# A Mamba scan and a mixture of experts on one core: the shared expert moved from 128-token tiles after the scan into the scan itself

## The chip, the cores and the metric

One core of a Trainium2 chip runs the program. The metric is the device time of one launch in microseconds; the kernel before takes 2628.02 us (median of 2 runs, 2627.62 to 2628.42). The engines are PE (TensorE, with its weight loads as PEld), DVE (VectorE), ACT (ScalarE), POOL (GpSimd) and SP (SyncE, which here only issues transfers). Each works through its own instructions in order and waits on semaphores.

## What is computed

```python
x = x + conv_ref(_ln_c(x), ...)     # Mamba: in_proj, 4-tap conv, scan over 2304 steps with 16 states, gate, out_proj
t = _to_tokens(x)                   # 4 images x 24 x 24 pixels = 2304 tokens of 512 channels
t = t + ffn_ref(_ln_t(t), ...)
# ffn: 8 experts (512 -> 1024 -> 512), the best two of each token, and one shared expert for all tokens
h1 = jnp.einsum('th,ehi->tei', xf, w1)
h3 = jnp.einsum('th,ehi->tei', xf, w3)
act = jax.nn.silu(h1) * h3
y = jnp.einsum('tei,te,eih->th', act, combine, w2)
shared = jnp.einsum('tni,nih->th', jax.nn.silu(s1) * s3, sw2)
return y + shared
```

All of it is float32.

## The kernel before

**The scan.** The sequence is cut into 24 chunks of 96 pixels (4 images, 6 chunks each; `g` is the chunk, `j` its place in the image, `b` the image). A chunk has 16 states, `n` = 0 to 15, and each engine's program walks over them. For one `n` ACT makes the decay `dA` (L868), DVE multiplies two halves of `dtu` with the spread B (L1110, L1112) and scans both halves (L1126), POOL multiplies with C (L612), and PE adds pairs of states into `Yt` (`add_pair`, L1454). B is spread by PE into two PSUM banks in turn (`spread`, L1444): the spread for pair `ph` + 2 stands in PE's program at `n` = 2 `ph` + 1, and DVE needs it at `n` = 2 `ph` + 4. Between these the program puts, at fixed `n`, the work of neighbouring chunks: the front half of chunk g + 1 and g + 2 (`dt_product`, `z_first`, `u_first`, `projections`, on ACT the silus at `n` = 2, `bc_hi` at 4 and `exps` at 7) and the back half of chunks g - 1 to g - 3 (`out_product`, the residual, layer norm, `row_transposes`, `gate_logits`). So the order on every engine is written out by hand in five functions named `batch`, one for each engine; ACT may run up to six states ahead of DVE (`AHEAD`), POOL up to six behind (`HRING`).

**The tiles.** After the last chunk the tokens are worked through in tiles of 128 rows with PE (L1581 up, L1593 down): first 18 tiles of all tokens in order with the shared expert's weights, then 43 tiles of rows gathered for the eight routed experts (`RTT` = 43, `NT` = 61). During the shared tiles DVE works out the routing (`softmax_and_greater`, `choose`, `weights_of_the_two`, `places`, `tables`), and POOL scatters the slots with 48 indirect transfers (L647). The shared tiles write their rows to `yrows`, the routed ones add to these rows (L678). At the end `yrows` is loaded, transposed and added to `X`, the residual, in SBUF.

The queue of SP carries nearly all transfers. In a chunk it issues, in this order, C, dt, the finished rows and dtu of the next chunk, each behind a wait of its own.

## Time and profile before

| stage of the profiled execution | us | granted clock (1.00 = 2.4 GHz) |
|---|---|---|
| set-up, until the first product for the scan | 93.9 | |
| scan of 24 chunks | 1105 | 0.77 to 0.85 |
| to the first shared tile | 24.4 | 0.64 |
| 18 shared tiles | 403.9 | 0.99 |
| 43 routed tiles | 956.3 | 1.00 |
| sum, transposes, output | 42.7 | 0.56 |
| span | 2626.3 | 0.884 |
| time of this execution | 2628.03 | |

The span runs from the first to the last instruction; 1.7 us lie around it. In the trace a float32 matmul stands as two instructions. Busy times of PE contain the filling and draining of matmuls that overlap, so a busy PE isn't necessarily at its limit.

### The profile page before, as it was taken

The page shows a single profiled execution, that of the slowest core. Times are in us where ns is not written, and L with a number is a line of the kernel's source. Part 1 is how long each engine was busy: PE and PEld are TensorE (multiplying, and loading weights), DVE is VectorE, ACT ScalarE, POOL GpSimd, SP SyncE. Part 2 cuts the span into 40 slices and gives each one's busy share as a digit, 9 for nine tenths or more (in the row PEclk, how much of TensorE's full clock was granted, in tenths as well). Part 3 has the DMA queues.
Part 4 walks back from the last instruction along what each step waited for, and adds up shares of the span by engine and source line. Part 5 has one row for each costly group of instructions (what it writes and reads, how often), then busy time and mean ns, then how long its engine had stood idle before and what let it go on. Part 6 is the DMA issues. An engine that isn't in the chain of part 4 may idle for free.

```text
span 2626.3 us, 28836 instructions
## 1 busy us (share of the span) xinstructions
PE 2252.7 (86%) x7604; PEld 1074.3 (41%) x7605; DVE 1312.3 (50%) x2049; ACT 1025.7 (39%) x2065; POOL 1213.6 (46%) x1133
## 2 busy tenths in 40 slices
PE   4577787777777787766999999999999999999995
PEld 3223433333333333323444444444444444444443
DVE  1599999999999999993321111111111111111112
ACT  2677787877878787761110011111111111101110
POOL 1689999999999999983042000011111111111110
PEclk7677878778788878867999999999999999999997
DMA  3433434344343443422003000332222232231116
GB/s 97 120 102 97 116 99 122 95 117 112 88 125 91 122 105 101 120 73 110 28 20 121 24 24 28 117 94 50 87 57 81 62 120 68 75 120 24 24 20 152
DMA packets 125077, 223.87 MB, mean 85 GB/s; under 512 B 16224, under 2 KB 95176, under 8 KB 122144
## 3 DMA queue, kind: packets, MB, share of 16 engines
q1 hardware_dynamic: 113760, 199.93, 26.3%
q0 software_dynamic: 11200, 22.63, 4.8%
q8 instruction: 42, 0.69, 0.1%
q14 instruction: 75, 0.61, 0.1%
HBM read 177.02 MB, written 45.50 MB: 85 GB/s over the span
## 4 chain that ended last, share of the span: by engine, by line
PE 53%; issue 13%; POOL 11%; ACT 9%; DVE 8%; DMA 5%; SPq 1%; POOLq 0%; ACTq 0%; DVEq 0%
PE pair L1581 28%; PE single L1593 16%; DVE WALL L1126 6%; POOL WALL L612 6%; DMA u<-xrows,gix 2%; ACT WALL L868 2%; PE single L1387 1%; POOL sp L520 1%; DMA u<-xrows 1%; ACT L706 1%; POOL sp L526 1%; PE pair L1345 1%; PE pair L1563 1%; PE pair L1604 1%; PE pair L1454 1%
## 5 line engine op out<-in xcount | busy, mean ns | idle before, releaser
L1581 PE MATMUL pair<-WALL,zz 128*128 (+1 forms) x1952 | 849.8, 593 | 2.0 <-ACT zz L934 2.0
L612 POOL TENSOR_TENSOR WALL<-WALL 128x768 f32<-128x768 f32 x384 | 692.6, 1813 | 47.1 <-DVE WALL L1126 45.9
L1126 DVE TENSOR_TENSOR_SCAN WALL<-WALL,carry,pair 128x384 f32<-128x384 f32 x640 | 609.9, 992 | 0.1
L1581 PEld LDWEIGHTS pair<-WALL,zz 128*128 128x128 f32 x1952 | 366.8, 190 | 441.5 <-issue 439.9
L868 ACT ACTIVATE WALL<-WALL,AnR 128x384 f32<-128x384 f32 x768 | 426.1, 604 | 41.2 <-DVE WALL L1126 28.4
L1593 PE MATMUL single<-WALL,sp 128*128 (+1 forms) x976 | 430.9, 594 | 2.9 <-issue 1.8
L940 ACT ACTIVATE zz<-pair 128x512 f32<-128x512 f32 x122 | 72.8, 597 | 813.7 <-PE pair L1581 813.7
L678 POOL DMA_INDIRECT yrows<-sp,aix x43 | 68.2, 1586 | 668.7 <-ACT sp L951 599.2
L1253 DVE SCALAR_TENSOR_TENSOR sp<-zz,tab,pair 128x512 f32<-128x512 f32 x86 | 64.3, 747 | 548.9 <-ACT zz L940 548.9
L1454 PE MATMUL pair<-WALL,fold 128*32 128x384 f32 x1536 | 213.3, 636 | 105.3 <-POOL WALL L612 101.0
L1593 PEld LDWEIGHTS single<-WALL,sp 128*128 128x128 f32 x976 | 181.3, 191 | 210.1 <-issue 210.1
L1262 DVE COPY sp<-pair 128x512 f32<-128x512 f32 x61 | 42.2, 692 | 393.4 <-PE pair L1604 393.4
L1112 DVE TENSOR_TENSOR pair<-WALL,pair 128x384 f32<-128x384 f32 x384 | 209.8, 546 | 0.0
L1110 DVE TENSOR_TENSOR pair<-WALL,pair 128x384 f32<-128x384 f32 x384 | 205.9, 536 | 6.6 <-DMA WALL<-dtd 6.6
L951 ACT ACTIVATE sp<-single 128x512 f32<-128x512 f32 x61 | 36.5, 598 | 389.6 <-PE single L1593 389.6
L1350 PE MATMUL single<-seq,Wu 128*128 128x384 f32 x384 | 168.2, 592 | 4.8 <-POOL seq L559 4.0
L1256 DVE TENSOR_TENSOR sp<-zz,pair 128x512 f32<-128x512 f32 x36 | 24.8, 688 | 217.6 <-ACT zz L940 217.5
L1444 PE MATMUL pair<-S,sel 96*128 96x384 bf16 x192 | 73.7, 385 | 68.0 <-DVE pair L1112 67.7
L664 POOL COPY gix<-tabi 128x1 int32 (+1 forms) x43 | 29.8, 692 | 209.0 <-PE pair L1563 209.0
L1350 PEld LDWEIGHTS single<-seq,Wu 128*128 128x128 f32 x384 | 85.0, 233 | 97.1 <-issue 66.5
L1126 DVE TENSOR_TENSOR_SCAN WALL<-WALL,h,pair 128x384 f32<-128x384 f32 x128 | 122.0, 992 | 0.0
L1454 PEld LDWEIGHTS pair<-WALL,fold 128*32 128x32 f32 x1536 | 33.4, 120 | 196.5 <-POOL WALL L612 159.3
(235 smaller groups left out, 2237.2 us busy)
## 6 DMA issues: line engine op xcount, KB each, us to landing
WALL<-dtd SPq DMA_DIRECT2D x384, 192.0 KB, 3.8
WALL<-in_L_ffn_w_dram SPq DMA_DIRECT2D x24, 2048.0 KB, 13.7
WALL<-crows SPq DMA_DIRECT2D x96, 192.0 KB, 3.5
dtd<-sp SPq DMA_DIRECT2D x96, 192.0 KB, 1.8
WALL<-in_L_ffn_sw_dram SPq DMA_DIRECT2D x3, 2048.0 KB, 12.1
X<-in_x_dram SPq DMA_DIRECT2D x4, 1152.0 KB, 6.6
xrows<-rows SPq DMA_DIRECT2D x24, 192.0 KB, 2.1
u<-xrows SPq DMA_DIRECT2D x18, 256.0 KB, 2.7
```

Of the source, the lines that this page charges most:

```text
L612: pool.tensor_tensor(hC[m], hs[:, (NS * j + n) % HRING, :, :], Cs[k][:, n % NPH // 2, :].unsqueeze(1).to_broadcast([P, HALF, T]), ALU.mult ...
L678: pool.indirect_dma_start(out=yrows, out_offset=bass.IndirectOffsetOnAxis(ap=aix[:, k:k + 1], axis=0), in_=yout[k], in_offset=None, comput ...
L868: a = nsc.activation(dA[(NS * j + n) % AHEAD][:, e, :], dtR[:, h * NQ + c + e, :], ACT.Exp, scale=AnR[:, c + e, h, q:q + 1])
L940: nsc.activation(sil[q], bank[q][:, :], ACT.Silu).then_inc(t_silu, 1)
L1110: nv.tensor_tensor(dBu[0], dtuR[:, h * NQ + c, :], Bq[:, 0:T], ALU.mult).then_inc(m_dBu0, 1)
L1112: nv.tensor_tensor(dBu[1], dtuR[:, h * NQ + c + 1, :], Bq[:, 0:T], ALU.mult).then_inc(m_dBu, 1)
L1126: scan = nv.tensor_tensor_scan(hs[:, m, e, :], dA[(NS * j + n) % AHEAD][:, e, :], dBu[e], init, ALU.mult, ALU.add)
L1350: last = mm((M0, M1)[h][:, 0:T], Wu[:, h, tap, :], seq[k][:, tap:tap + T], start=(tap == 0), stop=(tap == TAPS - 1))
L1444: mm(Bb[p % 2][:, 0:T], sel[:, p % NQ, :], S[j % 2][:, :], start=True, stop=True).then_inc(m_B, 1)
L1454: last = mm(Yt[c * DS:(c + 1) * DS, 0:T], fold[:, :], hC[(n - 1 + c // 2) % RING][:, c % 2, :], start=False, stop=(q == NQ - 1), tile_posi ...
L1581: last = mm(bank[2 * w + q][:, :], xT[k][:, r, :], WALL[:, ds(off + (w * RR * I + r * I + q * 512), 512)], start=(r == 0), stop=(r == RR - 1))
L1593: last = mm(bank[7][:, :], actT[c // 4][:, c % 4, :], WALL[:, ds(off + (2 * RR * I + c * C), C)], start=(c == 0), stop=(c == IK - 1))
```

## The change

The 18 shared tiles go. The shared expert is computed channel-major: weights are the stationary operand, and 288 normalised tokens (three chunks, a group) the moving one, straight from the layer norm's output (`XN`). A group takes three phases of eight pieces of 4 matmuls: w1 (copied by ACT into `act8`, then one silu over 2304 columns), w3 (multiplied into `act8` by DVE, `shared_gate`), and w2 (two pieces make one quarter of the channels; the residual is added with an identity matmul, and ACT, or DVE for the last quarter, copies the sum into `X`). Six of the eight groups are worked through in chunks 6 to 23, a phase to a chunk and a piece at every even `n`; the last two follow the scan. All pieces of the scan share one PSUM region, `E1`. The weights lie in DRAM as 24 pieces of 256 KB (`wsd`), copied there in the first chunks, and SP loads each into a ring of three. The 18 tiles' worth of rows in `yrows` are zeroed in the first chunks, and the 43 routed tiles add onto them.

To make room, `M2` (bank 1) becomes `E1`, and the statistics, row transposes and logits that used it go to `M1` at other places: transposes at PE's `n` = 2, their copy at ACT's `n` = 8, logits and mean at PE's `n` = 4, behind that copy; z moves from 4 and 7 to 6 and 8. The layer norm's last steps move to POOL's `n` = 14 and 15, and its reciprocal root to ACT's `n` = 3 of the next chunk. sw2 is loaded at the start and permuted by four DVE copies.

```diff
+                    def weights(q):
+                        if not first and not (last and j == JC - 1 and q + WRING >= PH):
+                            next_piece(b, j, q)
+                    if front:
                         store_c(g + 1, 1 - k, b * (JC // 2) + (j + 1) // 2)
+                    weights(0)
+                    if front:
                         load_c(g + 1, 1 - k)
+                    weights(1)
+                    weights(2)
+                    if not (first and j < 3):
+                        store_rows(g - 3, 1 - k)
+                    weights(3)
+                    if front:
                         store_dt(g + 1, 1 - k, 0)
                         spread_dt(g + 1, 1 - k, 0)
+                    weights(4)
+                    if front:
                         store_dt(g + 1, 1 - k, 1)
-                    if not (first and j < 3):
-                        store_rows(g - 3, 1 - k)
-                    if not (last and j == JC - 1):
+                    weights(5)
+                    if front:
                         store_dtu(g + 1, 1 - k, 0)
                         spread_dtu(g + 1, 1 - k, 0)
+                        spread_dt(g + 1, 1 - k, 1)
                         store_dtu(g + 1, 1 - k, 1)
-                        spread_dt(g + 1, 1 - k, 1)
...
+            for n in range(4, 2 * PH):
+                sp.wait_ge(e_ps, 3 * PH * LGRP + BATCH * (n - 3))
+                load_batch(n)
+                if n < 7:
+                    sp.dma_start(*first_set[n - 4]).then_inc(s_w, 16)
+                if n in (4, 5, 7):
+                    g = NCH - 3 + (n - 3) // 2
+                    store_rows(g, g % 2)
...
-                        if late and n == 11:
+                        if late and n == 14:
                             newton(g - 2, st2, b_st, b_y2, b_nw)
-                        if late and n == 12:
-                            normalise(g - 2, k)
+                        if late and n == 15:
+                            normalise(g - 2, lj)
...
+                        if not first:
+                            G, phase = group_of(b, j), j % GC
+                            if phase == 0 and n >= 4 and n % 2 == 0:
+                                h1_copy(G, n // 2 - 2, E1)
+                            if phase == 1 and n in (0, 2):
+                                h1_copy(G, n // 2 + 6, E1)
+                            if phase == 2 and n in (6, 10, 14):
+                                y_to_x(G, b - 1, j // GC, (n - 6) // 4, E1)
                         if n == 2:
                             if front:
                                 silu_u(g + 1, 1 - k)
-                            silu_z(g, j % 3)
+                            silu_z(g, k)
+                            if not first and j % GC == 1:
+                                shared_silu(group_of(b, j))
                             exp_and_ln()
-                        if late3 and n == 3:
-                            rows_copy(g - 3, 1 - k, M2)
+                        if late3 and n == 8:
+                            rows_copy(g - 3, 1 - k, M1)
...
+            def shared_gate(G, q, ps):
+                v.wait_ge(e_sil, G + 1)
+                v.wait_ge(e_ps, 3 * PH * G + PH + q + 1)
+                nv.tensor_tensor(act8[:, q, :], act8[:, q, :], ps, ALU.mult).then_inc(e_act, 1)
...
+                        if not first and j % GC == 1 and n % 2 == 0:
+                            shared_gate(group_of(b, j), n // 2, E1)
+                        if not first and j % GC == 2 and n == 14:
+                            v.wait_ge(e_ps, 3 * PH * group_of(b, j) + 3 * PH)
+                            nv.tensor_copy(xgroup(b - 1, j // GC, RR - 1), E1).then_inc(e_y, 1)
...
+            def up_piece(w, half, ps):
+                for r in range(RR):
+                    last = mm(ps, w[:, r, :], XN[half][:, r, :], start=(r == 0), stop=(r == RR - 1))
+                last.then_inc(e_ps, 1)
+
+            def down_piece(w, b, half, q, ps):
+                r, part2 = q // 2, q % 2
+                for kk in range(RR):
+                    last = mm(ps, w[:, kk, :], act8[:, part2 * RR + kk, :], start=(part2 == 0 and kk == 0), stop=False)
+                if part2 == 1:
+                    last = mm(ps, ident[:, :], xgroup(b, half, r), start=False, stop=True)
+                last.then_inc(e_ps, 1)
+
+            def piece(G, b, half, ph, q):
+                w = loaded(G, ph, q)
+                if ph == 0:
+                    if q == 0:
+                        pe.wait_ge(b_xn, GC * (G + 1))
+                        after(pe, e_y, RR * G)
+                    else:
+                        pe.wait_ge(e_h1, PH * G + q)
+                    up_piece(w, half, E1)
+                elif ph == 1:
+                    if q == 0:
+                        pe.wait_ge(e_h1, PH * (G + 1))
+                    else:
+                        pe.wait_ge(e_act, PH * G + q)
+                    up_piece(w, half, E1)
+                else:
+                    if q == 0:
+                        pe.wait_ge(e_act, PH * (G + 1))
+                    elif q % 2 == 0:
+                        pe.wait_ge(e_y, RR * G + q // 2)
+                    down_piece(w, b, half, q, E1)
...
                         if n == 0:
                             if front:
                                 dt_product(g + 1, 1)
+                        if n == 2:
+                            if front:
+                                dt_product(g + 1, 0)
+                            if late3:
+                                pe.wait_ge(f_abs, 2 * g + 3 if front else 2 * NCH)
+                                row_transposes(g - 3, (j - 3) % JC, M1)
+                        if n == 4:
                             if late3:
                                 pe.wait_ge(b_rows, g - 2)
-                                gate_logits(g - 3, 1 - k, M2)
+                                gate_logits(g - 3, (j - 3) % JC, M1)
+                            elif late:
+                                pe.wait_ge(f_abs, 2 * g + 3)
                             if late:
                                 pe.wait_ge(b_x, g - 1)
-                                mean_of(xchunk(lb, lj), b_mean, M2[:, STAT:STAT + CP])
-                        if front and n == 2:
-                            dt_product(g + 1, 0)
-                        if front and n == 4:
+                                mean_of(xchunk(lb, lj), b_mean, M1[:, STAT:STAT + CP])
+                        if front and n == 6:
+                            if late:
+                                pe.wait_ge(b_mc, g - 1)
                             z_first(g + 1, 1 - k)
-                        if front and n == 7:
+                        if front and n == 8:
                             z_second(g + 1, 1 - k)
...
-                        if n == 14:
-                            if front1:
-                                projections(g + 2, k)
-                            if late:
-                                if late3:
-                                    pe.wait_ge(b_log, g - 2)
-                                pe.wait_ge(b_mc, g - 1)
-                                row_transposes(g - 2, k, M2)
+                        if front1 and n == 14:
+                            projections(g + 2, k)
+                        if not first and n % 2 == 0 and n < 14:
+                            piece(group_of(b, j), b - 1, j // GC, j % GC, n // 2 + 1)
+                        if n == 14 and not (last if j == JC - 1 else first):
+                            if j == JC - 1:
+                                piece(group_of(b + 1, 0), b, 0, 0, 0)
+                            else:
+                                piece(group_of(b, j + 1), b - 1, (j + 1) // GC, (j + 1) % GC, 0)
...
+            for q in range(PH):
+                piece_last(L0, 1, q)
+            for q in range(2):
+                piece_last(L0, 2, q)
+            pe.wait_ge(b_rows, NCH - 1)
+            pe.wait_ge(b_log, NCH)
+            counts()
+            for q in range(2, PH):
+                piece_last(L0, 2, q)
+            for ph in range(3):
+                for q in range(PH):
+                    piece_last(L1, ph, q)
+            pe.wait_ge(r_cp, 1)
+            pe.wait_ge(b_rows, NCH)
+            pe.wait_ge(e_y, RR * NG)
             x_transpose(0, 0)
```

On PE, states `n` = 3 to 5 of the second chunk of the last image, before. `pair<-S,sel` is the spread of B, `WALL,fold` is `add_pair`, `seq,Wz` is z:

```order
L1444 MATMUL pair<-S,sel 128x384 [waits m_dBu]
L1451 MATMUL pair<-u,WALL 128x384 [waits b_gated]
L1454 MATMUL pair<-WALL,fold 32x384 [waits m_hC]
L1454 MATMUL pair<-WALL,fold 32x384 x3
L1372 MATMUL single<-seq,Wz 128x384 [waits f_abs_relu,m_dBu]
L1444 MATMUL pair<-S,sel 128x384 [waits m_dBu]
L1454 MATMUL pair<-WALL,fold 32x384 [waits m_hC]
L1454 MATMUL pair<-WALL,fold 32x384 x3
```

The same place after; `single<-gT,XA` are the logits, `single<-X,meanw` the mean, `pair<-XA,WALL 128x288` is a piece:

```order
L1614 MATMUL pair<-S,sel 128x384 [waits m_dBu]
L1621 MATMUL pair<-u,WALL 128x384 [waits b_gated]
L1624 MATMUL pair<-WALL,fold 32x384 [waits m_hC]
L1624 MATMUL pair<-WALL,fold 32x384 x3
L1519 MATMUL single<-gT,XA 96x8 [waits b_normalised,b_logits,b_rows_copied,m_dBu]
L1519 MATMUL single<-gT,XA 96x8 x3
L1446 MATMUL single<-X,meanw 128x96 [waits b_residual]
L1446 MATMUL single<-X,meanw 128x96 x3
L1533 MATMUL pair<-XA,WALL 128x288 [waits e_gated,e_piece_loaded2]
L1533 MATMUL pair<-XA,WALL 128x288 x3
L1614 MATMUL pair<-S,sel 128x384 [waits m_dBu]
L1624 MATMUL pair<-WALL,fold 32x384 [waits m_hC]
```

Where z stood alone between two spreads, now stand the logits, which wait for the copied rows, the mean, and a piece that waits for DVE's gate; the next spread is behind all of them.

On DVE, `n` = 3 and 4 of the same chunk before (`SCALAR_TENSOR_TENSOR` with `carry` is the scan, `yd` the gating of y):

```order
L1110 TENSOR_TENSOR pair<-WALL,pair 128x384 [waits m_h_half0_scanned]
L1112 TENSOR_TENSOR pair<-WALL,pair 128x384 [waits m_h_scanned]
L1073 TENSOR_TENSOR yd<-pair,zz 128x384 [waits b_out_in_psum,f_z_silu,m_y_added]
L1126 SCALAR_TENSOR_TENSOR WALL<-WALL,carry,pair 128x384 [waits m_carry_pair_copied,m_dBu_half0,m_hC,m_dA]
L1126 SCALAR_TENSOR_TENSOR WALL<-WALL,carry,pair 128x384 [waits m_dBu]
L1110 TENSOR_TENSOR pair<-WALL,pair 128x384 [waits m_h_half0_scanned,m_B_in_psum]
L1112 TENSOR_TENSOR pair<-WALL,pair 128x384 [waits m_h_scanned]
L1126 SCALAR_TENSOR_TENSOR WALL<-WALL,carry,pair 128x384 [waits m_carry_pair_copied,m_dBu_half0,m_hC,m_dA]
L1126 SCALAR_TENSOR_TENSOR WALL<-WALL,carry,pair 128x384 [waits m_dBu]
```

and after, with the gate of a piece (`XA<-XA,pair 128x288`) behind the two products and ahead of the scan:

```order
L1213 TENSOR_TENSOR pair<-WALL,pair 128x384 [waits m_h_half0_scanned]
L1215 TENSOR_TENSOR pair<-WALL,pair 128x384 [waits m_h_scanned]
L1166 TENSOR_TENSOR yd<-pair,zz 128x384 [waits b_out_in_psum,f_z_silu,m_y_added]
L1234 SCALAR_TENSOR_TENSOR WALL<-WALL,carry,pair 128x384 [waits m_carry_pair_copied,m_dBu_half0,m_hC,m_dA]
L1234 SCALAR_TENSOR_TENSOR WALL<-WALL,carry,pair 128x384 [waits m_dBu]
L1213 TENSOR_TENSOR pair<-WALL,pair 128x384 [waits m_h_half0_scanned,m_B_in_psum]
L1215 TENSOR_TENSOR pair<-WALL,pair 128x384 [waits m_h_scanned]
L1171 TENSOR_TENSOR XA<-XA,pair 128x288 [waits e_piece_in_psum,e_silu]
L1234 SCALAR_TENSOR_TENSOR WALL<-WALL,carry,pair 128x384 [waits m_carry_pair_copied,m_dBu_half0,m_hC,m_dA]
L1234 SCALAR_TENSOR_TENSOR WALL<-WALL,carry,pair 128x384 [waits m_dBu]
```

The gate waits for its piece on PE, and the scan of state 4 and everything later on DVE stand behind it.

On ACT, `n` = 2 to 4 of that chunk before (`u<-single,cb` and `zz<-zz` are the two silus, `rows` the copy of the rows, `dtr` and `S` the start of `bc_hi`):

```order
L714 ACT_TABLE_LOAD [waits f_dtu,m_D_u_added]
L714 ACTIVATE u<-single,cb 128x384 [waits f_u_in_psum] x2
L725 ACTIVATE zz<-zz 128x768 [waits f_z_copied]
L706 ACT_TABLE_LOAD
L868 ACTIVATE WALL<-WALL,AnR 128x384 [waits m_h_scanned]
L868 ACTIVATE WALL<-WALL,AnR 128x384
L800 ACTIVATE rows<-pair 96x512 [waits b_rows_stored1,b_transposed]
L868 ACTIVATE WALL<-WALL,AnR 128x384 [waits m_h_scanned]
L868 ACTIVATE WALL<-WALL,AnR 128x384
L812 ACTIVATE carry<-WALL 128x4 [waits m_h_scanned]
L732 ACTIVATE dtr<-single 8x384 [waits f_dt_in_psum,m_B_in_psum,f_bc_in_psum]
L733 ACTIVATE S<-single 96x384
```

and after, from the carry at `n` = 2 (`XA<-pair` is a copied piece, `XA<-XA 128x2304` the shared silu, `st` the layer norm's root):

```order
L894 ACTIVATE carry<-WALL 128x4 [waits m_h_scanned]
L879 ACTIVATE XA<-pair 128x288 [waits e_piece_in_psum]
L784 ACT_TABLE_LOAD [waits f_dtu,m_D_u_added]
L784 ACTIVATE u<-single,cb 128x384 [waits f_u_in_psum] x2
L795 ACTIVATE zz<-zz 128x768 [waits f_z_copied]
L883 ACTIVATE XA<-XA 128x2304 [waits e_h1_copied]
L776 ACT_TABLE_LOAD
L951 ACTIVATE WALL<-WALL,AnR 128x384 [waits m_h_scanned]
L951 ACTIVATE WALL<-WALL,AnR 128x384
L840 ACTIVATE st<-st 128x96 [waits b_variance_copied]
L843 ACTIVATE st<-st 128x96 [waits b_normalised,b_ln]
L845 ACTIVATE st<-st 128x96 [waits b_rsqrt]
```

A copy of the eighth w1 piece and the silu over 2304 columns now stand between that carry and `bc_hi`, which follows two states later; the copy of the rows is gone from here, and three steps of the layer norm are new.

## Rows read from the trace of the kernel before

**Rows 1.** The page's span in 40 slices: busy tenths by engine, granted clock.
```profile
PE   4577787777777787766999999999999999999995
DVE  1599999999999999993321111111111111111112
PEclk7677878778788878867999999999999999999997
```

**Rows 2.** Busy us (instructions) in stretches: us, engines, granted clock, DMA share, GB/s.
```profile
core 0: us, PE busy (x) PEld busy (x) DVE busy (x) ACT busy (x) POOL busy (x), PEclk, DMA share, GB/s
372.00:880.00 508.00, 393.00 (x1710) 187.17 (x1709) 499.65 (x756) 393.40 (x819) 471.95 (x407) 0.80 0.42 108
1268.00:1343.50 75.50, 74.66 (x204) 35.20 (x203) 32.46 (x88) 9.45 (x16) 0.00 (x0) 1.00 0.08 26
```

**Rows 3.** The chain that ended last: start us, us, what.
```profile
1203.89 17.51 DMA u<-xrows
...
1223.44 15.69 PE pair L1581 x32
...
1627.31 13.73 PE pair L1581 x32
...
1762.26 10.56 DMA u<-xrows,gix
...
2576.43 7.14 PE single L1593 x16
```

**Rows 4.** Timeline of DVE: start us, us, line, what, count [idle before, releaser].
```profile
93.86 0.56 DVE L1110 TENSOR_TENSOR pair<-WALL,pair 128x384 f32<-128x384 f32 x1 [6.60 <-DMA WALL<-dtd]
...
887.31 0.54 DVE L1110 TENSOR_TENSOR pair<-WALL,pair 128x384 f32<-128x384 f32 x1
887.75 0.55 DVE L1112 TENSOR_TENSOR pair<-WALL,pair 128x384 f32<-128x384 f32 x1
...
890.96 0.55 DVE L1112 TENSOR_TENSOR pair<-WALL,pair 128x384 f32<-128x384 f32 x1
...
901.47 0.54 DVE L1110 TENSOR_TENSOR pair<-WALL,pair 128x384 f32<-128x384 f32 x1
...
928.85 0.55 DVE L1066 TENSOR_TENSOR Rm<-single,S 64x384 f32<-64x384 f32 x1 [0.52 <-ACT bcrow L735]
...
1197.07 1.91 DVE L1126 TENSOR_TENSOR_SCAN WALL<-WALL,carry,pair 128x384 f32<-128x384 f32 x2
```

**Rows 5.** Timeline of ACT in the same chunk.
```profile
894.84 1.28 ACT L706 ACT_TABLE_LOAD   x1
896.13 1.12 ACT L868 ACTIVATE WALL<-WALL,AnR 128x384 f32<-128x384 f32 x2
...
922.50 0.84 ACT L725 ACTIVATE zz<-zz 128x768 f32<-128x768 f32 x1
...
925.69 0.57 ACT L800 ACTIVATE rows<-pair 96x512 f32<-96x512 f32 x1
```

**Rows 6.** Timeline of PE in the same chunk and behind the scan.
```profile
883.62 2.00 PE L1345 MATMUL pair<-X,meanw 128*128 x8
...
921.20 1.13 PE L1345 MATMUL pair<-WALL,meanw 128*128 128x96 f32 x8
...
928.83 0.84 PE L1417 MATMUL pair<-gT,WALL 128*96 128x8 f32 x8
...
1217.54 1.45 PE L1417 MATMUL single<-gT,WALL 128*96 128x8 f32 x8 [1.35 <-ACT rows L800]
```

**Rows 7.** Timeline of POOL: first slot scattered, slots back.
```profile
1343.75 1.14 POOL L647 DMA_INDIRECT slots<-pk,dsti  x1 [99.22 <-DVE WALL L1228]
...
1406.52 0.22 POOL L654 CAST tabi<-tab 128x43 int32<-128x43 f32 x1 [1.42 <-DMA tab<-slots]
```

**Rows 8.** The page's transfers by line: KB each, us from issue to landing.
```profile
WALL<-in_L_ffn_sw_dram SPq DMA_DIRECT2D x3, 2048.0 KB, 12.1
u<-xrows SPq DMA_DIRECT2D x18, 256.0 KB, 2.7
```

More of the change, by code:

```diff
@@ L403, in batch @@
+                    if first and j == 4:
+                        sp.wait_ge(s_wsd, 16 * (2 * PH + 1))
+                        for n in range(WRING):
+                            load_piece(n)
+                    weights(6)
+                    weights(7)
+                    if front:
                         spread_dtu(g + 1, 1 - k, 1)
             batches(sp, batch)
-            store_rows(NCH - 3, 1)
-            for k in range(2):
-                sp.wait_ge(b_out[k], 16 * (NCH // 2 - 2))
@@ L691, in _ @@
                     add_rows(2 * t2 + k, k)
-            gather(NT - 1, 0)
-            for t in range(NT - 3, NT):
+            gather(RTT - 1, 0)
+            for t in range(RTT - 3, RTT):
                 add_rows(t, t % 2)
@@ L1584, in up, with down @@
                     last.then_inc(t_h, 1)
[L1586 to L1587 removed]
+            def down(t):
+                off = set_of(t)
                 for q in range(2):
@@ L1647, in _ @@
-            with pe.Fori(SHT // 2, (NT - 3) // 2) as t2:
-                tile(2 * t2 + 1, 1, True)
-                tile(2 * t2 + 2, 0, True)
-            tile(NT - 2, 1, True)
-            tile(NT - 1, 0, True, ahead=False)
-            down(NT - 1, True)
+                    down(t - 1)
+                act_transpose(t)
+            for q in range(PH):
+                piece_last(L0, 1, q)
+            for q in range(2):
+                piece_last(L0, 2, q)
+            pe.wait_ge(b_rows, NCH - 1)
@@ new lines, in _ @@
+            pe.wait_ge(b_log, NCH)
[3 more added lines that the diff above has]
+            for ph in range(3):
+                for q in range(PH):
+                    piece_last(L1, ph, q)
+            pe.wait_ge(r_cp, 1)
+            pe.wait_ge(b_rows, NCH)
+            pe.wait_ge(e_y, RR * NG)
+            x_transpose(0, 0)
+            pe.wait_ge(r_done, 1)
+            tile(0, 0, behind=False)
+            tile(1, 1)
+            tile(2, 0)
@@ L1655, in _ @@
+            with pe.Fori(1, (RTT - 3) // 2) as t2:
+                tile(2 * t2 + 1, 1)
+                tile(2 * t2 + 2, 0)
+            tile(RTT - 2, 1)
+            tile(RTT - 1, 0, ahead=False)
+            down(RTT - 1)
             for g in range(NCH):
```

528 lines of the change are left out of this document (293 added, 235 removed).

## The prediction

> **What bounds the kernel now.** The span in slices comes first: PE is nine tenths busy from the 18th slice on, DVE from the 3rd to the 17th, and the granted clock of TensorE lies between 0.6 and 0.8 while DVE is full and at 0.9 and more after it [rows 1]. So there are two stages with different bounds. The busy times of the scan confirm it: of 508 us DVE is busy for 499.7, POOL for 472.0, PE and ACT for 393 each, at a mean clock of 0.80 [rows 2]. The scan runs from the first product at 93.9 to the end of the last scan at 1197.07 + 1.91 = 1199.0 [rows 4]: 1105.1 us for 24 chunks, 46.05 each. Behind it the chain is PE's alone. The first shared tile begins at 1223.4, the first routed one at 1627.3, and the last down product ends at 2576.43 + 7.14 = 2583.6 [rows 3]. The 18 shared tiles thus take 403.9 us, the 43 routed ones 956.3, the rest of the span (2626.3) 42.7.
>
> In a chunk PE is busy for 393.0 / 508 x 46.05 = 35.6 us. At the clock of 0.80 that is 28.5 us of work at full clock.
>
> **What is removed and what is added.** Between the scan and the first routed tile lie 1627.3 - 1199.0 = 428 us, and these are rebuilt.
>
> *A piece.* At full clock a tile's 32 up instructions with 512 columns take 13.73 us [rows 3], 0.429 each; with 288 columns 0.241. A piece of four matmuls is eight such, 1.93 us; a group has 24 pieces and 4 more matmuls, 48.3 us; a chunk of the scan gets a third of it, 16.1 us. Six groups go into chunks 6 to 23, two behind the scan (96.6 us).
>
> *DVE in the scan.* Two products of 384 columns start 0.44 us apart [rows 4]. A gate with 288 columns costs between 0.33 (in proportion) and 0.44; I take 0.35. Nine for a group, six groups: 19 us. DVE is the bound there, so this counts in full.
>
> *The wait at `n` = 4.* PE's logits now wait for rows that ACT copies at `n` = 8. ACT's `n` = 8 begins at 896.1, behind `exps` and its table load; two decays, a carry and the copy (0.57) end it near 897.9 [rows 5]. DVE had finished the products of `n` = 4 at 891.5 and starts those of `n` = 8, which need the next spread, at 901.5 [rows 4]. Behind the rows PE has logits, mean and a piece ahead of that spread: at full clock 0.84 + 1.13 + 1.93 = 3.9 us, so the spread comes at about 902.3, 0.8 too late; at the low level 1.45 + 2.00 + 3.86 = 7.3 and the spread doubled, 905.9, 4.4 too late [rows 6]. PE stands idle ahead of it, which favours the low level. I take 2.5 for the first and third phase, the middle. In the second phase DVE itself waits for that piece, at its gate of `n` = 6, two states earlier: its products end near 896.9 (2.74 us a state, 2 x 2.74 + 0.45 behind 890.96 [rows 4]), the piece at 901.8 or 905.2: 4.9 to 8.3 less what DVE's three gates have taken by then (1.05); I take 5. The spread then comes in time.
>
> *The silu of 2304 columns.* 768 columns take 0.84 us [rows 5]; three times as many at most 2.5, I take 2.3. It stands on ACT, with a copied piece (0.4), ahead of `bc_hi`, for which DVE already waited 0.52 us at `n` = 1 in one chunk [rows 4]. What is queued behind DVE's residue is the whole scan. Between 0 (ACT has run ahead) and 5 (the last w1 piece is late too), I take 4.
>
> So a group costs 2.5 in its first phase, 2.8 + 4 + 5 = 11.8 in its second (eight gates), 2.5 + 0.35 in its third: 17.2 us, and six groups **103 us**.
>
> *What I cost at nothing.* Copies on ACT (11 a group) lie in its idle quarter [rows 2]. The later layer norm makes POOL wait for ACT's `n` = 3; cover is POOL's idle 7%, 3.3 us a chunk, and without it the wait would reach `add_pair` and the scan. SP's loads are 8 x 256 KB a chunk, 2.1 MB in 46 us, 45 GB/s beside 108 at a DMA share of 0.42 [rows 2]: about 0.60, an estimate. One lands in 2.7 us [rows 8] and is issued three pieces, six states or 16 us, ahead; if SP stood behind the row store for longer, the piece and the spread behind it would be late. Zeroing and splitting the weights go into the first six chunks on the same queue, and the spread of dtu behind them has eight states, 22 us.
>
> *Set-up.* The 2 MB of sw2 stand ahead of the small vectors: three such together took 12.1 us [rows 8], 4 each. Bounds 0 and 12; I take **4**. Its permuting on DVE falls where DVE is a tenth busy [rows 1].
>
> *Behind the scan.* Before, the second last chunk's logits were done at 1219.0, 20 us after the scan [rows 6]; the last chunk's need one more norm between pieces: 30 (25 to 40). Then the routing, with no shared tiles to cover it: DVE was busy for 32.5 us in that stretch, some 8 of it for tiles [rows 2], so 24; eight gates 2.8; waits for pieces and counts 7: 64. Bounds 24 and the 75.5 it took. Scattering the slots and reading them back took 1343.75 to 1406.74 [rows 7], 63: 127. A gather among weight loads took 10.6 us [rows 3], and the second expert's weights are now issued just when the last group is done: 138. From rows landed to the first up product 1223.44 - 1221.40 = 2.0 [rows 3]: **140** (131 to 160). PE is done with both groups at about 20 + 96.6 + 8 = 125, so its work is covered by the chain over POOL, and it idles.
>
> *Routed tiles.* Unchanged but for one down product of a shared tile in the first: 956.3 - 7.1 = **949.2**. The end stays 42.7.
>
> Sum: 1199.0 + 4 + 103 + 140 + 949.2 + 42.7 = 2437.9 of span. The profiled execution took 2628.03 with a span of 2626.3, 1.7 more, and lies on the median of 2628.02: **2440 us**.
>
> **The rivals.**
>
> *Everything hides but DVE's own work.* ACT and PE adapt, and a chunk grows by 1.05 us: 2440 - 84 = 2356. For it: weight loads keep PE busy for only 187 of 508 us [rows 2], so much of its 393 is filling and draining. Against: PE waits in order behind ACT's `n` = 8. The Trainium skill (Perfetto Trace Analysis, section Identifying the Most-Contended Engine) calls matmul busy time a poor measure and LDWEIGHTS busy the better one; by this rule there is room for the pieces, and 2356 is what it gives.
>
> *PE becomes the bound at today's clock.* 28.5 + 16.1 = 44.6 us of work at full clock, at 0.80 55.8 a chunk, 9.7 more, 18 x 9.7 = 175 instead of 103: 2512. For it: waits between pieces stay, as PE's idle time does now. Against: the tiles, where PE never waits, run at 0.9 and more [rows 1]. The Trainium skill (TensorE: Matmul & The Clock Gate, section HAM oscillation) says that pauses between bursts of matmuls throw the clock back to half; the slices agree (0.6 to 0.8 in the scan).
>
> *The shared work isn't hidden at all.* Pieces and scan alternate, each chunk grows by 16.1: 2440 - 103 + 290 = 2627, no change. It needs DVE to stop for every piece; DVE waits for a piece only in one phase of three.
>
> *Slower: TensorE stays at its low level in the whole scan.* 44.6 us become 89 a chunk, 43 more: 2440 - 103 + 18 x 43 = 3111. It decides from 2681 on, a chunk of 65.2 us, which is a clock of 0.68 with PE never idle. Against it speaks 0.80 with less work.
>
> **How the numbers follow.** The forecast has 0.52, the first rival 0.17, the second 0.25, no change 0.03, slower 0.03. 2% is about what a measurement can tell from no change. Faster by over 2% means under 2575, which the forecast and two rivals are: 0.94; within 2% 0.03; slower 0.03. The forecast's own range is 2395 to 2490 (waits at their low and high ends). The range to 8 in 10 takes in both neighbours: 2350 to 2515.
>
> **What the new profile would show.** Chunks of 6 to 23 in a rhythm of three, about 48.5, 58 and 49 us; DVE idle ahead of gates and of the residue in the second, ahead of products of `n` = 8 in the others; PE waiting for ACT's row copy at `n` = 4. Behind the scan some 140 us to the first up product, ended by POOL and a gather, with PE idle at the end. Routed tiles as before. Wrong would be: even chunks near 47 (first rival), PE without idle time at a clock near 0.8 (second), or a first up product at over 160.

## The result and the profile after

The changed kernel takes 2514.84 us (median of 2 runs, 2514.68 to 2514.99) against 2628.02 before: a ratio of 0.957 (95% interval 0.953 to 0.961), 113 us less. The forecast was 2440. The sign was right, and the time lies in the range by 0.16 us; 75 us of the 188 that were forecast didn't come.

The page's slices answer to [rows 1]. From the 7th slice to the 21st, where the pieces are in the scan, DVE falls to seven or eight tenths in most slices and PE rises to eight: no engine is full any more, which points at waits between engines. The granted clock stands at 0.8 to 0.9 there, above that of the old scan.

```profile
PE   4577778888888888888877878999999999999995
DVE  2499998887987888879887401111111111111112
...
PEclk7676788988988989989988999999999999999997
```

Busy times by stage answer to [rows 2]: the scan, from its end to the first routed product, and the routed tiles (us; busy us and count of PE, PEld, DVE, ACT, POOL; granted clock, DMA share, GB/s).

```profile
100.00:1366.30 1266.30, 1040.06 (x4762) 603.23 (x4762) 1118.84 (x1703) 873.55 (x1803) 1016.41 (x851) 0.87 0.50 129
1366.30:1516.89 150.59, 114.80 (x492) 89.01 (x493) 34.29 (x104) 21.56 (x47) 56.99 (x68) 0.87 0.48 165
1516.89:2470.20 953.31, 946.90 (x2576) 444.39 (x2576) 119.70 (x172) 97.66 (x170) 123.54 (x166) 1.00 0.23 63
```

Term by term, the sum of the forecast stands against the trace so:

| term | forecast, us | measured, us | missing |
|---|---|---|---|
| scan begins | 97.9 | 100.0 | 2.1 |
| scan | 1105 + 103 | 1266.3 (+161) | 58 |
| scan end to first routed product | 140 | 150.6 | 10.6 |
| routed tiles | 949.2 | 953.6 | 4.4 |
| end, and outside the span | 44.4 | 44.2 | -0.2 |

(The last down product ends at 2470.5, 0.3 us behind the window of the last row.) Three quarters of the miss lie in the scan. Chunks 0 to 5 take 45.4 us, 45.6 before. From chunk 6 on there is the rhythm of three that was forecast, but larger: a first phase takes 50.3, a second 62.0, a third 55.7 us (here and below, means over the first five groups), where 48.5, 58 and 49 were expected. The last group, in whose chunks the work for chunks to come runs out, takes 48.4, 59.9 and 45.5. Chunks 12 to 14 in busy times:

```profile
710.64:761.27 50.63, 43.66 (x199) 26.84 (x199) 45.99 (x71) 30.66 (x67) 39.31 (x33) 0.87 0.49 127
761.27:823.16 61.89, 52.07 (x233) 31.64 (x233) 48.95 (x78) 42.40 (x84) 44.11 (x38) 0.89 0.46 117
823.16:878.30 55.14, 48.57 (x230) 30.29 (x228) 46.23 (x71) 38.79 (x82) 43.96 (x39) 0.91 0.50 128
```

DVE, the bound of old, has 46 to 49 us of work in each and waits for the rest. What it waits for is in its timeline (start us, us, line, operation; in brackets the idle time before and what ended it): in a first phase the products of `n` = 8 and 10, in the second the gate of `n` = 0, the residue at `n` = 1, the gates of `n` = 2, 6 and 8 (0.79, not in the lines), in the third, besides what the first has, the copy of the last quarter at `n` = 14.

```profile
735.76 0.56 DVE L1213 TENSOR_TENSOR pair<-WALL,pair 128x384 f32<-128x384 f32 x1 [2.18 <-PE pair L1614]
...
742.49 0.56 DVE L1213 TENSOR_TENSOR pair<-WALL,pair 128x384 f32<-128x384 f32 x1 [1.15 <-PE pair L1614]
...
765.32 0.46 DVE L1171 TENSOR_TENSOR XA<-XA,pair 128x288 f32<-128x288 f32 x1 [3.02 <-PE pair L1533]
...
770.31 0.55 DVE L1159 TENSOR_TENSOR Rm<-single,S 64x384 f32<-64x384 f32 x1 [1.79 <-ACT bcrow L805]
...
775.28 0.46 DVE L1171 TENSOR_TENSOR XA<-XA,pair 128x288 f32<-128x288 f32 x1 [1.68 <-PE pair L1533]
...
793.19 0.45 DVE L1171 TENSOR_TENSOR XA<-XA,pair 128x288 f32<-128x288 f32 x1 [5.66 <-PE pair L1533]
...
873.29 0.46 DVE L1227 COPY X<-pair 128x288 f32 x1 [3.56 <-PE pair L1541]
```

PE, for which DVE waits, has itself stood idle a little earlier. In chunk 12 it is done with `n` = 3 at 723.5 and starts the logits 5.5 us later:

```profile
722.72 0.85 PE L1624 MATMUL pair<-WALL,fold 128*32 128x384 f32 x8
729.04 1.45 PE L1519 MATMUL single<-gT,XA 128*96 128x8 f32 x8 [5.46 <-DVE pair L1215]
730.34 2.00 PE L1446 MATMUL single<-X,meanw 128*128 x8
732.13 3.43 PE L1533 MATMUL pair<-XA,WALL 128*128 128x288 f32 x8
735.39 0.33 PE L1614 MATMUL pair<-S,sel 96*128 96x384 bf16 x1
```

The row names DVE as the releaser, but the products of `n` = 4 had long been done. The wait for several semaphores ended with ACT's copy of the rows, at 728.27 + 0.58, which stands behind the exponentials and their table loads:

```profile
725.56 1.28 ACT L776 ACT_TABLE_LOAD   x1
726.85 1.12 ACT L951 ACTIVATE WALL<-WALL,AnR 128x384 f32<-128x384 f32 x2
...
728.27 0.58 ACT L870 ACTIVATE rows<-single 96x512 f32<-96x512 f32 x1
```

The logits and the mean then run at the low level of the clock (granted 0.50; 1.45 and 2.00, as in the old rows of that level [rows 6]), the piece for the most part too (granted 0.60; 3.43), so the spread for `n` = 8 follows 6.4 us after the logits' start. From there PE works without a pause to the end of the chunk: it is late in everything that it does after `n` = 4. What it had to do in the five idle microseconds it can't make up.

### The profile page after: what moved, and what is told of

It is laid out like the page before. It is cut to its first block, busy times and chain, and to the rows that moved or that the text cites. A ratio compares the mean times of both kernels' runs of the same rounds, so it can differ in the third digit from the quotient of the medians.

```text
span 2512.9 us, 30004 instructions
## 1 busy us (share of the span) xinstructions
PE 2163.7 (86%) x8124; PEld 1181.8 (47%) x8125; DVE 1300.5 (52%) x2051; ACT 1031.0 (41%) x2087; POOL 1220.7 (49%) x1133
## 4 chain that ended last, share of the span: by engine, by line
PE 55%; DVE 16%; issue 12%; ACT 6%; DMA 5%; POOL 4%; SPq 1%; DVEq 0%; POOLq 0%; ACTq 0%
PE pair L1773 20%; PE single L1785 12%; DVE WALL L1234 11%; PE pair L1533 5%; PE single L1451 3%; DMA u<-xrows,gix 3%; PE pair L1539 2%; PE single L1446 2%; POOL slots L718 2%; DVE pair L1215 2%; PE pair L1624 2%; ACT WALL L951 1%; POOL WALL L683 1%; PE single L1519 1%; PE single L1473 1%
## 5 line engine op out<-in xcount | busy, mean ns | idle before, releaser
L1773 PE MATMUL pair<-WALL,zz 128*128 x1376 | 599.3, 593 | 1.8 <-ACT zz L1049 1.0
L1773 PEld LDWEIGHTS pair<-WALL,zz 128*128 128x128 f32 x1376 | 258.7, 191 | 311.8 <-issue 311.8
L1363 DVE SCALAR_TENSOR_TENSOR sp<-XA,tab,pair 128x512 f32<-128x512 f32 x86 | 64.3, 747 | 591.6 <-ACT XA L1055 591.6
L1533 PE MATMUL pair<-XA,WALL 128*128 128x288 f32 x1024 | 306.2, 452 | 9.7 <-DVE XA L1171 9.7
L1785 PE MATMUL single<-WALL,sp 128*128 x688 | 303.1, 593 | 2.7 <-issue 1.5
L1055 ACT ACTIVATE XA<-pair 128x512 f32<-128x512 f32 x86 | 51.4, 597 | 578.8 <-PE pair L1773 578.8
L1533 PEld LDWEIGHTS pair<-XA,WALL 128*128 128x128 f32 x1024 | 214.9, 214 | 89.2 <-issue 19.8
L1785 PEld LDWEIGHTS single<-WALL,sp 128*128 128x128 f32 x688 | 127.4, 190 | 148.8 <-issue 148.8
L1624 PE MATMUL pair<-WALL,fold 128*32 128x384 f32 x1536 | 177.6, 537 | 17.6 <-POOL WALL L683 12.3
L1539 PE MATMUL pair<-XA,WALL 128*128 128x288 f32 x512 | 150.9, 445 | 5.1 <-DVE pair L1215 2.9
L1539 PEld LDWEIGHTS pair<-XA,WALL 128*128 128x128 f32 x512 | 104.8, 209 | 43.7 <-DVE pair L1215 7.8
L1519 PE MATMUL single<-gT,XA 128*96 128x8 f32 x176 | 30.1, 299 | 101.5 <-issue 58.5
```

The lines of the kernel that those rows point to most:

```text
L1533: last = mm(ps, w[:, r, :], XN[half][:, r, :], start=(r == 0), stop=(r == RR - 1))
L1539: last = mm(ps, w[:, kk, :], act8[:, part2 * RR + kk, :], start=(part2 == 0 and kk == 0), stop=False)
L1624: last = mm(Yt[c * DS:(c + 1) * DS, 0:T], fold[:, :], hC[(n - 1 + c // 2) % RING][:, c % 2, :], start=False, stop=(q == NQ - 1), tile_posi ...
L1773: last = mm(bank[2 * w + q][:, :], xT[k][:, r, :], WALL[:, ds(off + (w * RR * I + r * I + q * 512), 512)], start=(r == 0), stop=(r == RR - 1))
L1785: last = mm(bank[7][:, :], actT[c // 4][:, c % 4, :], WALL[:, ds(off + (2 * RR * I + c * C), C)], start=(c == 0), stop=(c == IK - 1))
```

## The experiments

The theory: the scan grows by waits between engines, above all PE's wait for the row copy at `n` = 4, and by PE's lateness behind it. The main rival: PE simply has too much to do, 48.1 us busy in a mean chunk of 55.9, so that a wait that is taken away comes back elsewhere.

**The row copy earlier.** The changed kernel, with one instruction of ACT in another place:

```diff
                         if front and n == 7:
                             abs_relu(g + 1, 0)
+                        if late3 and n == 7:
+                            rows_copy(g - 3, 1 - k, M1)
+                        if front and n == 7:
                             exps(g + 1)
-                        if late3 and n == 8:
-                            rows_copy(g - 3, 1 - k, M1)
```

> ACT copies the transposed rows at n = 7, ahead of the exponentials, instead of at n = 8; nothing else changes. Theory (a wait at PE's n = 4): the 5.3 us that PE stands idle ahead of the logits in each chunk go. The next wait is at PE's n = 6, where z waits for the copy of the mean at ACT's n = 10, so about 3.5 of the 9.8 us that a chunk grew by come back: 18 x 3.5 = 63, 2452 us. Rival (PE's work is the bound): PE is busy for 48.1 of 55.9 us of a chunk, what it idles here it idles elsewhere, and the time stays above 2500.

Measured: 2455.33 us, 59.5 less. PE's idle time ahead of the logits fell to 1.0, and the gate of the second phase that found its piece late is now that of `n` = 8, at 2.7 us instead of 5.7 at `n` = 6:

```profile
703.53 0.84 PE L1520 MATMUL single<-gT,XA 128*96 128x8 f32 x8 [1.00 <-DVE pair L1216]
...
772.09 0.46 DVE L1172 TENSOR_TENSOR XA<-XA,pair 128x288 f32<-128x288 f32 x1 [2.73 <-PE pair L1534]
```

The logits take 0.84 us at a granted clock of 1.00, the high level. The rival's 2500 is excluded.

**The mean's copy earlier too.** ACT's copies of the logits and the mean move in one piece:

```diff
                         if front and n == 8:
                             bc_mid(g + 1, 1 - k)
+                        if n == 8:
+                            if late:
+                                sc.wait_ge(b_mean, g - 1)
+                            if late3:
+                                logits(g - 3, M1)
+                            if late:
+                                mean_copy(g - 2, mcp2, M1[:, STAT:STAT + CP], b_mean, b_mc, b_cen)
-                        if n == 10:
...
```

> As e1_rows_early, and ACT's copies of the logits and the mean stand at n = 8 instead of n = 10. Theory (waits of PE for ACT): z at PE's n = 6 no longer waits either, DVE finds its spreads of n = 8 and 10 in time, and the gate of n = 6 finds its piece; what stays is the second phase's start (silu, about 7 us) and some of the third phase's copy at n = 14: 5.4 us a chunk come back, 97 in all, 2418 us. Rival (PE's work): above 2490.

Measured: 2419.65 us, 95.2 less than the changed kernel, with the same work on every engine. The three phases take 47.5, 54.9 and 48.4 us. Chunks 12 to 14:

```profile
673.66:720.97 47.31, 42.60 (x199) 25.54 (x199) 45.88 (x71) 30.78 (x68) 39.70 (x33) 0.89 0.51 137
720.97:776.48 55.51, 49.02 (x233) 29.18 (x233) 48.85 (x79) 42.24 (x83) 43.84 (x38) 0.94 0.49 130
776.48:825.19 48.71, 45.97 (x230) 28.07 (x228) 45.99 (x72) 38.32 (x83) 43.89 (x39) 0.96 0.56 146
```

PE's matmuls are the same in number (199, 233, 230) and PE's busy time fell from 144.3 to 137.6 while the clock rose from a mean of 0.89 to 0.93. How much of the 95 us comes from the shorter waits and how much from the faster clock behind them no run separates. First and third phase are now within 2.5 us of the old chunk; the second keeps what lies at its start.

**Less work, the wait kept.** The other half of the question, on the changed kernel itself; `few` is 1 for the pieces of the scan, and `down_piece` is changed alike:

```diff
-                for r in range(RR):
-                    last = mm(ps, w[:, r, :], XN[half][:, r, :], start=(r == 0), stop=(r == RR - 1))
+                for r in range(few):
+                    last = mm(ps, w[:, r, :], XN[half][:, r, :], start=(r == 0), stop=(r == few - 1))
```

> The changed kernel, with one matmul instead of four in each piece of the scan (the sums over channels are left out for these six groups); order and waits stay. Theory (the wait at n = 4, with the piece behind it): the wait stays at about 5 us on PE, but what stands behind it is shorter by 2.5 us, so a first phase is 3 us shorter, a second 6, a third 8 (its last piece is in time): 17 a group, 103 in all, 2412 us. Rival (PE's work alone): the chunks fall to 46.1 plus DVE's gates, about 47.3, and the time to 2365. If pieces cost little and the moved statistics all, it stays above 2460.

Measured: 2401.41 us, 113.4 less. The phases take 46.1, 54.0 and 47.3 us, although PE waits ahead of the logits nearly as before:

```profile
686.06 1.45 PE L1519 MATMUL single<-gT,XA 128*96 128x8 f32 x8 [4.43 <-issue]
687.36 2.00 PE L1446 MATMUL single<-X,meanw 128*128 x8
689.15 1.22 PE L1533 MATMUL pair<-XA,WALL 128*128 128x288 f32 x2
```

So in a first phase the wait alone costs nothing (46.1 against 46.05 of old), and the work alone costs little (47.5 without the wait). It is the two together that make PE late.

The second phase takes 54 to 55 us in both, but not for the same reason. With full work and without the wait, the gate of `n` = 6 is in time, and the gates of `n` = 0 and 2 and the residue wait 3.02, 1.68 and 1.78 us. With a quarter of the work and the wait, the gates of `n` = 0 and 2 find their pieces ready, the residue waits 2.09, and the gate of `n` = 6 still waits 2.85 behind the logits:

```profile
715.21 0.45 DVE L1171 TENSOR_TENSOR XA<-XA,pair 128x288 f32<-128x288 f32 x1
...
720.50 0.55 DVE L1159 TENSOR_TENSOR Rm<-single,S 64x384 f32<-64x384 f32 x1 [2.09 <-ACT bcrow L805]
...
738.78 0.46 DVE L1171 TENSOR_TENSOR XA<-XA,pair 128x288 f32<-128x288 f32 x1 [2.85 <-PE pair L1533]
```

So the lateness at the start of the second phase comes in part from PE's matmuls and in part from ACT, and that the two totals agree is chance.

**The copy at `n` = 14.** One number is changed, on the changed kernel:

```diff
-                        if not first and j % GC == 2 and n == 14:
+                        if not first and j % GC == 2 and n == 15:
                             v.wait_ge(e_ps, 3 * PH * group_of(b, j) + 3 * PH)
                             nv.tensor_copy(xgroup(b - 1, j // GC, RR - 1), E1).then_inc(e_y, 1)
```

> DVE's copy of the last quarter stands at n = 15 instead of n = 14 in every third chunk. Theory: the 3.5 us that DVE waits there for the last piece of the phase go, the copy takes place at the same time as now and the next piece is not later: 6 x 3.4 = 20, 2494 us. Rival: PE's first piece of the next phase waits in its place, and DVE's next products behind that: no gain, 2512 to 2517.

Measured: 2505.22 us (one run), 9.6 less, between the two; the scan is 8.7 shorter in the trace. A third phase falls from 55.7 to 53.1, the first phase behind it grows from 50.3 to 50.9, and there a residue now waits for ACT:

```profile
867.34 0.46 DVE L1227 COPY X<-pair 128x288 f32 x1 [0.82 <-PE pair L1541]
...
874.31 0.55 DVE L1159 TENSOR_TENSOR Rm<-single,S 64x384 f32<-64x384 f32 x1 [0.87 <-ACT bcrow L805]
```

The wait was real; a part of it moves on to the next phase.

**The start of the second phase.** In the changed kernel ACT waits 3.76 us at `n` = 2 for the eighth w1 piece, and everything of that chunk's front half stands behind it. From here on the kernel of the second experiment (2419.65) is the base. The copy goes behind the two silus that don't need it:

```diff
-                            if phase == 1 and n in (0, 2):
-                                h1_copy(G, n // 2 + 6, E1)
+                            if phase == 1 and n == 0:
+                                h1_copy(G, 6, E1)
...
                             silu_z(g, k)
                             if not first and j % GC == 1:
+                                h1_copy(group_of(b, j), 7, E1)
                                 shared_silu(group_of(b, j))
```

> e2_both_early, and in a second phase ACT's copy of the eighth w1 piece stands behind the two silus of n = 2 instead of ahead of them. Theory (at the start of a second phase ACT stands 3.8 us at that copy for PE's piece, and its silus, B and C of the next chunk, DVE's residue and the gate of n = 2 are late by that): the table load and two silus run in the wait, and 0.9 + 1.8 + 1.7 = 4.4 us a group come back, 26 in all, 2394 us. Rival (the silu of 2304 columns alone makes them late): no gain, 2415 to 2420.

Measured: 2401.94 us, 17.7 less than the base. The wait shrinks to 0.63, DVE's residue waits no more, and the gates at `n` = 0 and 2 wait 1.92 and 0.62 instead of 3.02 and 1.68 (of the base they are the same as those shown of the changed kernel):

```profile
713.82 0.41 ACT L879 ACTIVATE XA<-pair 128x288 f32<-128x288 f32 x1 [0.63 <-PE pair L1535]
...
719.07 0.45 DVE L1173 TENSOR_TENSOR XA<-XA,pair 128x288 f32<-128x288 f32 x1 [1.92 <-PE pair L1535]
726.11 0.45 DVE L1173 TENSOR_TENSOR XA<-XA,pair 128x288 f32<-128x288 f32 x1 [0.62 <-PE pair L1535]
```

A second phase falls from 54.9 to 51.4. The gate of `n` = 0 was expected to lose 0.9 and lost 1.1; that of `n` = 2 kept 0.6, and a first phase grew by 0.5. That is where the 26 us fell short.

**The silu's length.** Same base; `few` is 1 in the scan:

```diff
-                nsc.activation(act8[:, :, :], act8[:, :, :], ACT.Silu).then_inc(e_sil, 1)
+                nsc.activation(act8[:, 0:few, :], act8[:, 0:few, :], ACT.Silu).then_inc(e_sil, 1)
```

> e2_both_early, with the silu in the scan over 288 of its 2304 columns (seven eighths are left out for these six groups): ACT gets 1.8 us back ahead of B and C. Theory (one chain of copy, silus and table load, where each microsecond counts): DVE's residue comes 1.8 us earlier and the gate of n = 2 is in time, 1.8 to 3.5 us a group, 11 to 21 in all, 2399 to 2409 us. Rival (the silu is covered by ACT's lead): 2418 to 2420.

Measured: 2402.64 us, 17.0 less. ACT still waits 3.76 at the copy, the silu takes 0.44 instead of 2.12 us:

```profile
716.75 0.41 ACT L879 ACTIVATE XA<-pair 128x288 f32<-128x288 f32 x1 [3.76 <-PE pair L1534]
...
720.16 0.44 ACT L883 ACTIVATE XA<-XA 128x288 f32<-128x288 f32 x1
```

So copy, silus and table load are one chain ahead of `bc_hi`: 1.7 us taken out of it bring 2.8 us a group (17.0 / 6). The silu isn't covered, as the theory of this run had it, and the copy's wait isn't the only thing that makes the chain late.

**The two ends.** Same base, two orders of SP's queue:

```diff
             load_x(0, s_x0)
-            sp.dma_start(hs_all[:, 0:IK * C].rearrange("p (k n) -> p k n", k=IK),
-                         sw2[0].rearrange("(k p) n -> p k n", p=P)).then_inc(s_w2, 16)
...
             for b in range(1, B):
                 load_x(b, s_x)
+            sp.dma_start(hs_all[:, 0:IK * C].rearrange("p (k n) -> p k n", k=IK),
+                         sw2[0].rearrange("(k p) n -> p k n", p=P)).then_inc(s_w2, 16)
...
             for n in range(4, 2 * PH):
                 sp.wait_ge(e_ps, 3 * PH * LGRP + BATCH * (n - 3))
-                load_batch(n)
-                if n < 7:
-                    sp.dma_start(*first_set[n - 4]).then_inc(s_w, 16)
                 if n in (4, 5, 7):
                     g = NCH - 3 + (n - 3) // 2
                     store_rows(g, g % 2)
+                load_batch(n)
+                if n > 8 and n < 12:
+                    sp.dma_start(*first_set[n - 9]).then_inc(s_w, 16)
```

In the changed kernel the chain of waits behind the scan (start us, us, what) shows what this is about. Two stores of 192 KB take 9.8 and 9.3 us each, issued behind two loads of 768 and 2048 KB of weights:

```profile
1386.09 9.76 DMA xrows<-rows
...
1396.56 9.25 DMA xrows<-rows
...
1440.94 1.14 POOL slots L718
...
1498.82 5.73 DMA slots<-pk,dsti
...
1516.89 15.44 PE pair L1773 x32
```

> e2_both_early, with two orders of SP's queue changed outside the scan: sw2 is loaded behind the small vectors and the images, and behind the scan the rows are stored ahead of the weight loads, the second set of routed weights being issued later. Theory (loads ahead in the queue): the scan begins at 94, 5 us earlier, and the two row stores of 9 to 10 us take 2 to 3, which brings the routing about 6.5 us forward: 2419.7 - 11.5 = 2408 us. Rival (stores wait for their rows, the vectors are not late for sw2): 2417 to 2420. The first routed product can't come earlier by more than the logits of the last chunk allow, so 15 us would be too much.

Measured: 2406.90 us, 12.8 less. DVE's first product starts at 93.0, as before the change [rows 4], 6.0 earlier than in the base (99.0), and from the scan's end to the first routed product it takes 143 us instead of 150.7. The timeline of DVE:

```profile
93.01 0.56 DVE L1214 TENSOR_TENSOR pair<-WALL,pair 128x384 f32<-128x384 f32 x1 [6.45 <-DMA WALL<-dtd]
```

The stores behind the scan, in the list of transfers for that stretch (KB each, median us from issue to landing), now take 2.5 us and are gone from the chain:

```profile
xrows<-rows SPq DMA_DIRECT2D x3, 192.0 KB, 2.5
```

**All of it.** The edits of the first, second, fourth, fifth and seventh experiment together:

> e5_copy_behind, e7_ends and the copy of e4_copy15 together. If their gains add up: 2419.7 - 26 - 11.5 - 10 = 2372 us; if the same slack is counted twice at n = 14 and 15 and the next phase's start, 2380 to 2385.

Measured: 2373.58 us (median of 4 runs, 2371.76 to 2374.45), a ratio of 0.903 to the kernel before (0.902 to 0.905). The total is the 2372 of the forecast, but its parts are not: the three gains as they were measured one by one (17.7, 12.8 and 9.6) would give 2379.6, and together they brought 6 us more. No run shows where these come from. The scan and chunks 12 to 14:

```profile
92.59:1230.80 1138.21, 983.62 (x4762) 555.54 (x4762) 1114.05 (x1703) 869.84 (x1803) 1013.54 (x853) 0.92 0.55 144
...
656.79:703.52 46.73, 42.01 (x201) 25.40 (x202) 45.77 (x70) 35.28 (x73) 41.09 (x34) 0.93 0.53 136
703.52:754.30 50.78, 45.72 (x232) 27.30 (x230) 48.68 (x78) 39.09 (x81) 43.71 (x38) 1.00 0.56 145
754.30:800.20 45.90, 42.97 (x224) 26.21 (x224) 45.90 (x71) 37.12 (x79) 43.20 (x37) 1.00 0.61 157
```

DVE is busy for 1114 of 1138 us again. The scan is 33 us longer than before the change, of which DVE's own 54 new instructions (48 gates at 0.37 and 6 copies) make some 20.

## Why the prediction was right and where it fell short

**Right:** the stages and their bounds, the idle time of PE ahead of the first routed product (23.5 us), what the pieces cost at full clock (sixteen behind the scan in a row take 31.2 us, 1.95 each; 1.93 was worked out), the set-up's mechanism, the DMA share (0.53 to 0.61 in the last kernel's chunks, 0.60 estimated), and each of the waits that were named: the logits behind the row copy, the gate of `n` = 6 (5.7 us against 5), the residue. From the first scatter to the first routed product the chain takes 76.0 us, where 75.4 was worked out, but here two misses cancel: the slots are back and converted after 68.8 instead of 63, and gather and first product then take 7.1 instead of 12.6. One reading of [rows 1] was off without consequence: PE is at nine tenths from the 20th slice on, not from the 18th.

**The term that failed is the scan: 103 us worked out, 161 measured.** It failed in three steps. In each of the first five groups they cost 12.7 us more than the 17.2 of the forecast, 63 in all; the last group cost 1.5 less than forecast, and chunks 0 to 5 are together 3.8 shorter than six mean chunks of old: 58.

*The wait at `n` = 4 was followed to one product only.* The prediction asked when the spread for `n` = 8 comes, took the middle between the two clock levels, 2.5 us, and stopped there. The measured wait at that product is 1.5 to 2.5 in first phases and 2.8 to 2.9 in third ones, so the number was good, though partly by luck: in chunks 12 and 14 the clock was at its low level over the logits and the mean, for which the prediction had 4.4, but the rows were copied 5.3 and 5.6 us behind DVE's products of `n` = 4 instead of 6.4, and from the logits to the spread it took 6.4 and 6.8 us instead of 7.3. But PE has no slack behind it, and the next spread is late too (1.15 us at `n` = 10), and the gating of y behind that. The prediction's own question, what is late next, was put for DVE and not for PE. A first phase costs 4.2 us more than the old chunk of 46.05 instead of 2.5.

*The copy at `n` = 14 was priced as an instruction.* It got 0.35 us, DVE's own time. It is the only place of the third phase where DVE waits for a piece, and the last piece of the phase stands in PE's program at `n` = 12, at the end of PE's lateness: 3.56 us of idle time. A third phase costs 9.7 us more than the old chunk instead of 2.85; half of the missing 6.8 us is this wait, the rest the lateness of the first step again. The wait stood in the diff. For the gates of the second phase the same question had been asked, but not for this copy.

*The start of the second phase was sized at 4 us, with 5 as its upper bound, and is 6.8* (in chunk 13 the three states `n` = 0 to 2 take 16.2 us where they take 8.7 in chunk 12; two gates of 0.37 are counted elsewhere). The silu itself was right (2.12 against 2.3). What was missing is the wait of ACT at the copy ahead of it, 3.76 us, where the prediction had counted the copy's own time, and the gate of `n` = 2, which waits for a piece that stands in PE's program behind a product that needs `bc_hi`:

```profile
769.49 1.61 PE L1488 MATMUL single<-dtr,Wd 8*128 8x384 f32 x2 [3.26 <-ACT dtr L802]
```

**The second rival gave 2512, and it is not what happened.** It took a clock of 0.80 and PE without idle time. The trace has 0.87 to 0.91 in these chunks, PE idle for 5.5 us at one place, and with the same matmuls and three instructions of ACT moved the time falls by 95 us. Its agreement with the measured time is a coincidence, which the experiments show. The first rival (everything hides but DVE's work, 2356) was wrong for this kernel too; with the waits taken out the same work comes within 18 us of it. So the rule on contended engines that was weighed there (the Trainium skill, Perfetto Trace Analysis, section Identifying the Most-Contended Engine) pointed the right way about PE: in the last kernel PE's matmuls are busy for 42 to 46 us of chunks of 46 to 51, its weight loads for 25 to 27, and DVE is still busy for 98% of the scan. What it can't show is an order in which PE waits. The logits after 5.5 us of idle time take 1.45 us, after 1.0 us 0.84. With these two rows the rule that was weighed for the second rival agrees (the Trainium skill, TensorE: Matmul & The Clock Gate, section HAM oscillation). The pause just ahead doesn't decide alone: the old kernel's logits behind the scan took 1.45 after 1.35 us [rows 6].

**The smaller terms.** The set-up cost 6.1 instead of 4: sw2 stood ahead of the small vectors and delayed all of them, and behind them it costs nothing. Behind the scan the chain is 10.6 us longer, all of it ahead of the first scatter (74.6 against 64), of which the two row stores explain 7.7 (the experiment on the two ends); the prediction had the logits of the last chunk at 30 us (32.4 measured) and no store between them and the softmax. The copy of the rows waits for the store ahead of it, and the softmax's exponential stands behind that copy on ACT. The routed tiles cost 4.4 us more: the first one's up products take 15.44 instead of 13.73, at a granted clock of 0.91 behind PE's idle time, and PE then waits 1.5 us (0.60 and 0.86) ahead of the second tile's up products, where before a shared tile's down product stood.

## What to carry to other kernels

When an instruction is made to wait in an in-order engine, don't stop at the first consumer: add up what that engine still has to do until it next has slack, and price every later hand-over by that lateness. Each new instruction that reads another engine's result gets two prices, its own time and the lateness of what it reads; here the place of one copy of 0.58 us was worth 59.5 us, and a DVE copy of 0.46 us waited for 3.56. And before a merge of two workloads is judged by busy times, look for the two or three instructions that tie their orders together: moving three copies on an engine that was about two thirds busy brought back 95 us, where the whole change had brought 113.

## What the runs showed of the hardware

TensorE's granted clock rose with the work that was added, and again when waits were taken out, which the forecast had not counted on. The old scan as a whole, in the trace of the kernel before:

```profile
93.90:1199.00 1105.10, 830.20 (x3566) 385.01 (x3566) 1093.73 (x1649) 836.27 (x1731) 1012.98 (x853) 0.78 0.41 104
```

Its mean is 0.78, that of the changed kernel's scan 0.87, and that of the last one 0.92, with chunks at 1.00. Chunks 12 to 14 with a quarter of the pieces' work show less than with all of it:

```profile
667.96:714.28 46.32, 38.64 (x168) 19.97 (x172) 45.65 (x70) 34.08 (x71) 40.70 (x34) 0.74 0.54 142
714.28:768.21 53.93, 40.46 (x172) 19.90 (x164) 48.75 (x79) 39.60 (x81) 43.34 (x37) 0.81 0.51 132
768.21:815.03 46.82, 40.12 (x190) 20.80 (x188) 46.16 (x72) 37.43 (x81) 43.26 (x37) 0.85 0.59 152
```

Work that fills PE's pauses is thus partly paid for by the clock: a third more matmul records (4762 against 3566) keep PE busy for 984 us in the last kernel's scan, 18% more than the 830 of before.

Stores of 192 KB took 9.3 to 9.8 us behind the two weight loads in the same queue and 2.5 us ahead of them.
